# Graph attention with layer norm on one core: reciprocals spread by a DRAM round trip instead of TensorE, and division straight out of the weighed bank

## The reference

```
q, k, v = x Wq', x Wk', x Wv' + bv          (12 heads of 32)
a = q k' * 384**-0.5 + adj                  (per head, adj the same for all heads)
a = -inf in rows that are all 0;  a = softmax(a);  a = 0 where it is not a number
o = (a v, heads side by side) Wo' + bo
out = (r - mean(r)) / sqrt(var(r) + 1e-5),  r = x + o
```

## Time and profile before

| | us |
|---|---|
| median of 3 runs | 717.3 (717.02 to 719.97) |
| the profiled execution | 718.51 |
| its span, first to last instruction | 716.2 |
| PE busy in it | 698.7 |
| ACT busy | 613.8 |
| DVE busy | 600.1 |
| POOL busy | 487.2 |

### The profile page before, as it was taken

The page is one execution under the profiler, slowest core; times in us unless marked ns, Lnnn a source line. Parts: engine busy times, 40 slices in busy tenths (PEclk is TensorE's granted clock), DMA queues, the critical chain, the costliest instruction groups (busy, mean ns, idle before and its releaser), DMA issues.

```text
span 716.2 us, 23143 instructions
## 1 busy us (share of the span) xinstructions
PE 698.7 (98%) x7557; PEld 600.7 (84%) x7557; DVE 600.1 (84%) x2220; ACT 613.8 (86%) x1993; POOL 487.2 (68%) x548
## 2 busy tenths in 40 slices
PE   8999999999999999999999999999999999999895
PEld 8878888888888888888888888888898888888774
DVE  4898988889888889888889888889888889888973
ACT  4889988889988889988888988889888888898882
POOL 4767666677766678766677766678766677766452
PEclk9999999999999999999999999999999999999998
DMA  8475877787777687777787777787777777777672
GB/s 266 152 278 206 300 267 264 252 315 236 263 263 273 241 309 240 265 264 267 251 302 240 262 267 259 252 305 247 257 270 261 262 291 248 255 273 259 248 288 90
DMA packets 84008, 184.61 MB, mean 258 GB/s; under 512 B 4272, under 2 KB 42928, under 8 KB 75696
## 3 DMA queue, kind: packets, MB, share of 16 engines
q1 hardware_dynamic: 83888, 183.12, 72.3%
HBM read 103.42 MB, written 79.69 MB: 256 GB/s over the span
## 4 chain that ended last, share of the span: by engine, by line
PE 85%; DVE 5%; DMA 4%; issue 2%; POOL 2%; ACT 1%; SPq 0%; DVEq 0%; ACTq 0%; POOLq 0%
PE bank_b L787 34%; PE bank_c L787 16%; PE bank_a L877 12%; PE s_bank L836 11%; PE bank_t L847 8%; PE bank_c L858 2%; DVE neg L1192 2%; DMA sq_dram<-w_f 2%; DMA sq_probT<-sq_dram 2%; ACT prob L559 1%; PE bank_t L858 1%; DVE w_f L1209 1%; DMA xt<-in_xT 1%; POOL kq_lo L400 0%; DVE y L1292 0%
## 5 line engine op out<-in xcount | busy, mean ns | idle before, releaser
L559 ACT ACTIVATE prob<-neg,negmax 128x256 f32<-128x256 f32 x768 | 380.3, 500 | 51.8 <-DVE w_f L1209 34.3
L1192 DVE CUSTOM_DVE_ANT_0 neg<-s_bank,bias_sq 128x256 f32<-128x256 f32 x512 | 185.2, 414 | 49.0 <-issue 42.6
L1209 DVE STREAM_TRANSPOSE w_f<-prob 128x512 f32<-128x512 f32 x256 | 173.2, 696 | 0.7 <-ACT prob L559 0.7
L559 ACT ACTIVATION_READ_ACCUMULATOR prob<-neg,negmax 128x1 f32 x768 | 147.7, 192 | 0.0
L400 POOL TENSOR_TENSOR kq_lo<-kq,kq_hi 128x512 fp32r<-128x512 f32 x96 | 125.2, 1304 | 7.7
L398 POOL CAST kq_hi<-kq 128x512 fp32r<-128x512 f32 x96 | 60.2, 627 | 79.3 <-issue 73.9
L787 PE MATMUL bank_c<-xt_hi,w_hi 128*128 128x256 f32 x384 | 111.1, 289 | 1.0 <-DVE w_lo L1171 1.0
L787 PE MATMUL bank_c<-xt_hi,w_lo 128*128 128x256 f32 x384 | 108.3, 282 | 0.0
L787 PE MATMUL bank_c<-xt_lo,w_hi 128*128 128x256 f32 x384 | 108.3, 282 | 0.0
L1192 DVE CUSTOM_DVE_ANT_0 neg<-s_bank,bias 128x256 f32<-128x256 f32 x256 | 91.0, 420 | 15.2 <-PE s_bank L836 15.0
L847 PE MATMUL bank_t<-ident,prob 128*128 128x128 f32 x512 | 80.3, 279 | 0.7 <-ACT probT L569 0.7
(11 more groups left out here) (88 smaller groups left out, 1794.1 us busy)
## 6 DMA issues: line engine op xcount, KB each, us to landing
sq_dram<-w_f SPq DMA_DIRECT2D x64, 1024.0 KB, 4.5
sq_probT<-sq_dram SPq DMA_DIRECT2D x64, 1024.0 KB, 5.6
xt<-in_xT SPq DMA_DIRECT2D x32, 384.0 KB, 4.5
xr<-in_x SPq DMA_DIRECT2D x32, 384.0 KB, 6.2
out_y<-y_out SPq DMA_DIRECT2D x31, 384.0 KB, 3.0
bias<-in_adj SPq DMA_DIRECT2D x32, 256.0 KB, 3.2
w_f<-in_wkT SPq DMA_DIRECT2D x3, 192.0 KB, 4.5
w_f<-in_wqT SPq DMA_DIRECT2D x3, 192.0 KB, 5.0
```

The costliest lines, as they stand in the source:

```text
L559: nc.scalar.activation(prob[:, u % PROB_RING, k], neg[:, h, w.c], ACT.Exp, scale=-1.0, bias=negmax[t.p][:, w.c, h:h + 1], accum_out=sums[t ...
L1192: nc.vector.tensor_tensor_reduce(out=neg[:, h, w.c], in0=s_bank[h % JH][:, w.c, :], in1=by[t.p][:, w.c, :], scale=-1.0, scalar=BIG, op0=AL ...
L1209: nc.vector.transpose(sq_stage[w.g][:, :, a:a + PAIR, :, w.c].rearrange("p b h m s -> p (h m) b s"), prob[:, u % PROB_RING].rearrange("p k ...
```

## The change

It has four parts.

1. `widen_inv` (POOL) and `spread` (PE) go. `sums` is laid out so that the reciprocals of a row block, 24 columns of a 128 x 32 tile, can be transposed by DVE in blocks of 32 (`turn_inv`), stored to DRAM (`store_inv`, 16 KB) and loaded again by four DMAs, each of which gives 32 partitions the same row of 768 values (`load_inv`, inv_all).
2. `divide` now takes one g at a time, straight out of bank_a, and multiplies with inv_all. `save_o` goes, and o_n has two copies. The next weighing waits for the division (`o_n_ready`) instead of the copy.
3. v's second half is copied out by ACT (`copy_v`) and gets bv from POOL (`add_bv`); the first half stays with DVE. The flag moves from bank_a to bank_t.
4. The written order of all five engines is new, and the loop runs over batches 3 to 28. K01 is projected two batches ahead, x is loaded three ahead.

```diff
-    sums = [sb(f"sums{p}", [P, NT, H]) for p in range(2)]
+    sums = [sb(f"sums{p}", [P, JH, KC, NT]) for p in range(2)]
...
-    flags_at = bank_a[:, N:N + NT * H]
+    flags_at = t_flat[:, 0:NT * H]
...
+            def store_inv(t):
+                sp.wait_ge(inv_turned, t.count(1, 1))
+                apart(sp)
+
+                after(sp, inv_loaded[t.p], JH * (t.loads() - DMA))
+                sp.dma_start(inv_dram[t.p].rearrange("k b r -> b k r"),
+                             inv_t[:]).then_inc(inv_stored[t.p], DMA)
+
+            def load_inv(t):
+                sp.wait_ge(inv_stored[t.p], t.loads())
+                apart(sp)
+
+                after(sp, o_n_ready, t.count(KC, -KC))
+                for j in range(JH):
+                    row = inv_dram[t.p][KC * NT * j:KC * NT * (j + 1)].rearrange("k b r -> (k b r)")
+                    sp.dma_start(inv_all[t.p][HD * j:HD * (j + 1)].rearrange("p g n -> p (g n)"),
+                                 row.rearrange("(a n) -> a n", a=1).to_broadcast([HD, KC * N])
+                                 ).then_inc(inv_loaded[t.p], DMA)
...
+            def add_bv(t):
+                pool.wait_ge(b_loaded, 2 * DMA)
+                pool.wait_ge(v_copied, t.count(1, 1))
+                apart(pool)
+                nc.gpsimd.tensor_tensor(v[t.p][:, 1, :], v[t.p][:, 1, :], bv_all[:], ALU.add).then_inc(v_saved[1], 1)
...
-            def save_o(t, g):
-                act.wait_ge(pv_done[g], t.count(1, 1))
-
-                after(act, o_n_ready, t.count(2, -2))
-                nc.scalar.activation(o_raw[t.p][:, g, :], bank_at(t, f"PV{g}")[:, 0:N], ACT.Copy).then_inc(o_saved[g], 1)
+            def copy_v(t):
+
+                act.wait_ge(v_done, t.count(NT, 2))
+
+                for g in range(KC):
+                    after(act, pv_done[g], t.count(1, -1))
+                nc.scalar.activation(v[t.p][:, 1, :], bank_at(t, "V1")[:, 0:D], ACT.Copy).then_inc(v_copied, 1)
...
+            def turn_inv(t):
+                dve.wait_ge(inv_ready, t.count(1, 1))
+
+                if t.c >= 1:
+                    dve.wait_ge(inv_stored[1 - t.p], t.later(-1).loads())
+                apart(dve)
+                nc.vector.transpose(inv_t[:], inv[:]).then_inc(inv_turned, 1)
+
+            def divide(t, g):
+                dve.wait_ge(pv_done[g], t.count(1, 1))
+                if g == 0:
+                    dve.wait_ge(inv_loaded[t.p], JH * t.loads())
+
+                    after(dve, o_ready, t.count(2, -2))
+                    apart(dve)
+                nc.vector.tensor_tensor(o_n[t.p][:, g, :], bank_at(t, f"PV{g}")[:, 0:N], inv_all[t.p][:, g, :],
+                                        ALU.mult).then_inc(o_n_ready, 1)
```

More of the change, by code:

```diff
@@ new lines, in start @@
+                pe.wait_ge(kq_saved["Q12"], t2.count(1, 1))
+                project_kq(t3, "K01")
+                copied(t0, 11)
+                flag(t1)
+                pe.wait_ge(o_n_ready, t0.count(KC, 1))
+                weigh(t0, 1)
+                scores(t2, 0)
+                pe.wait_ge(flag_read, t1.count(1, 1))
+                transposes(t1, 8)
+                pe.wait_ge(o_n_ready, t0.count(KC, 2))
+                weigh(t0, 2)
+                pe.wait_ge(kq_saved["K2Q0"], t3.count(1, 1))
@@ L1069, in end @@
                 t31 = Batch(31)
+                scores(t29, 2)
+                copied(t28, 10)
+                transposes(t28, 11)
+                pe.wait_ge(kq_saved["K2Q0"], t30.count(1, 1))
+                project_v(t29, 1)
+                pe.wait_ge(kq_saved["K01"], t30.count(1, 1))
+                project_kq(t30, "Q12")
+                pe.wait_ge(o_n_ready, t28.count(KC, 1))
+                weigh(t28, 1)
+                pe.wait_ge(v_copied, t29.count(1, 1))
+                project_y(t27, 0)
```

794 lines of the change are left out of this document (427 added, 367 removed).

## The result

The changed kernel takes **747.8 us** (median of four runs, 740.70 to 753.59), the kernel before 717.2 in the same session: a ratio of 1.038, 95% interval [1.034, 1.041]. (Ratios are taken from the executions within 1.5% of a kernel's fastest alone: here three of the four, with a median of 746.4.) The forecast was 697 us with a range of 691 to 712. It is wrong, in sign too.

The account below looks back on a forecast made before the run. PE, busy all through the steady loop, was taken as the bound. From 718.5 us, 32 batches times 0.61 (19.5) and 1.0 for the end came off, giving 698.0; 1.2 less for the runs' median gave 697 us, range 691 to 712.

Parts of the forecast that it names:

- PE's step of 20.84: PE's new order in the steady loop, priced piece by piece: 20.84 us per step instead of 21.45, bounds 20.6 to 21.0.
- DVE's 0.4 us of margin: DVE's walk through the loop: no PE wait, the tightest place being the second division before weigh 2, 0.4 us to spare.
- part 6: Start and end of the kernel: 1.0 us off for the end, between 2.5 off and 2.5 on top.
- the factor of 32: The sum over the whole kernel: all 32 batches counted at 0.61 us saved each, 19.5 us.
- ACT and POOL were worth nothing: The two helper engines with copies and additions moved between them: enough time to spare, nothing counted.
- The second rival: DVE's margin is not there and PE waits at weigh 2: 707 us, or 717 if 0.6 us late; range 703 to 713.7, chance 0.14.
- part 4: The reciprocals' way through DRAM: 8.0 us from turn to landing, against about 9.3 that PE can bear.
- hidden, by 1.3 us: The reciprocals' way through DRAM costs PE nothing, with 1.3 us to spare.
- not full: DMA engines in the shorter step: 0.4 MB more per batch takes the busy share from 0.75 to about 0.83.
- the 1 MB load loses 1 us at most: SP's queue: the squares' load, waiting for a squares' store of 4.5 us, is delayed by at most 1 us.
- The first rival: Reciprocals reach DVE late, PE waits at weigh 1: 757 us, or 735 at a way of 10.5 us; chance 0.08 (slower).
- The rule on the store: Reciprocals' store to DRAM: slowest dimension 4, so 4 DMA engines; matters only if it lands after the squares ahead of the loads.

Follow-up runs that it names:

- e6: Changed kernel with the reciprocals' store and SP's waits kept, but the four loads left out from batch 3 on: 701.15 us.
- e1: Changed kernel with the reciprocals' store and four loads issued for the first two batches only: 700.28 us.
- e5: Changed kernel with, from batch 3 on, only the four loads, into a tile nobody reads, without the store and SP's waits for it: 747.52 us.
- e8: Changed kernel with the reciprocals' store and four loads issued by ACT on its own queue, SP's order otherwise kept: 851.11 us.
- e7: Changed kernel with SP's order changed: squares' load before the reciprocals' store, both x loads between store and four loads: 738.00 us.
- e12: Changed kernel with SP's whole step reordered so other transfers cover each landing, x transposed loaded four batches ahead; right data: 735.43 us.
- e9: As e5, changed kernel with loads into an unread tile and no store, but two of the four loads: 732.00 us.
- e11: As e5, but the 384 KB read as 128 different rows of x in one DMA to 128 partitions: 733.42 us.
- e18: Changed kernel with all orders and waits kept, but x's 384 KB for the residual not loaded from batch 2 on: 717.45 us.
- e17: Changed kernel with e12's order on SP and e14's on DVE, the four loads issued by GpSimd's queue in the loop: 743.40 us.
- e13: e12 with the four loads going to a tile nobody reads from batch 3 on, DVE dividing by batch 2's reciprocals: 729.12 us.
- e14: e12 with DVE inverting and turning the reciprocals earlier, behind two of the next batch's four bias additions: 735.48 us.
- e4: Changed kernel with the four loads ahead of the second load of squares in SP's order: 796.13 us.
- e2: Changed kernel with store and SP's waits kept, but from batch 3 on the four loads go to a tile nobody reads: 749.75 us.
- e15: e12 with the four loads made one DMA of 128 partitions, same bytes and rows, outermost dimension 4: 811.57 us.
- e3: Changed kernel with the reciprocals' store cut into four DMAs of 32 partitions: 761.86 us.

## Why the prediction was wrong

**What held.** PE's step of 20.84, with the spread's 0.59 us in it (20.83 and 20.86 in e6 and e1, PE busy 500 of 500 us), and DVE's 0.4 us of margin: in e6 the second division ends at 300.81 and the third weighing starts at 301.29. Without the loads no wait of PE shows, and both runs stand at 700 to 701 us, within the forecast's own 693 to 703 though 3 to 4 over its number. Those 3 to 4 lie outside the loop. Its 26 steps, 0.61 shorter each, give 15.9 of the 17.2 us between the profiled executions (718.51 and 701.33), which leaves 1.3 for start and end; part 6 and the factor of 32 counted 4.7. ACT and POOL were worth nothing, as said. The second rival (DVE's margin) did not occur.

**The step that failed** is in part 4: "its busy share of 0.75, in a shorter step too, to about 0.83: not full", and with it "hidden, by 1.3 us". The four loads were taken for traffic that costs nobody anything; they cost 46 us (e5 against e6). Three things in it were wrong.

*The size of the term.* Busy share times mean step is the time that a step's packets take on all 16 DMA engines; with shares read to two places it is good to about 0.1 us. Without the loads it is 0.77 x 20.83 = 16.0 us (e6), the same as before, 0.75 x 21.45 = 16.1. In the changed kernel it is 0.83 x 22.24 = 18.5. The forecast added 384 KB at the stage's mean rate per busy engine, 265/0.75 = 353 GB/s, so 1.1 us. They take **2.4 us**, over twice that. It is no constant of these bytes: with the same four loads it is 1.6 in e8 (0.66 x 26.7), 1.8 in e7 (0.81 x 22.0) and 2.2 in e12 (0.83 x 22.0). In e9 half of the loads adds 0.80 x 22.18 - 16.0 = 1.7; in e11 the same bytes in one transfer 0.81 x 22.24 - 16.0 = 2.0.

Of the 2.4 us, the loads' own packets are 128 x 195 ns / 16 = 1.6; with e11's 126 ns they would be 1.0, about what was forecast. The other 0.8 are packets of the old transfers that became longer: those of 1536 bytes (x for the residual and the output) from 71 ns in e6 to 83, those of 2048 (the squares' loads) from 101 to 107.

In the forecast's step of 20.84 the share would have to be 0.89, not 0.83. It reads 0.83 because the step grew. A packet's time counts its waiting too (119 ns at the least, 195 on average), so the 18.5 is no pure demand; but e6 and before agree at two step lengths. And e18, with e6's bytes but four narrow loads in the place of one wide one, has 0.79 x 21.62 = 17.1: for the same bytes the narrow form adds 1.0 us.

*What "not full" means.* No run got past 0.83 and 279 GB/s between 100 and 600 us: the changed kernel 273, e17 276, e12 277, e7 and e13 278, e14 279, with several orders and two queues. The rate needed in a step of 20.84 is e6's 275 plus 384 KB in 20.84 us (19), 294 GB/s. So a mean of 0.83 was the most that was reached here, not 1.00. That it is the capacity of the engines is not shown, and it isn't the whole: e9 (0.80, 266 GB/s) and e18 (0.79, 263) stay below it, and below e6's 275, and are still 31 and 13 to 16 us slower than e6. There landings close a loop with SP's waits, as e14's chain has it, and a reordering moved 12 us.

*Landings taken as constants.* The 5.6 us of the earlier trace rows was kept for the squares' load, and 4.5 for their store ("the 1 MB load loses 1 us at most"). The squares' store went to 7.9, and from e6 (5.3) to there only the loads and DVE's wait for them were added. The store itself did not slow down: one of its packets, 8192 bytes, takes 313 ns on average, 315 in e6. But from its issue to its first packet lie 3.4 and 3.6 us (medians of the two stores of a step), 0.8 and 1.5 in e6. SP runs late and issues its transfers closer together, so what went ahead is still under way: the first store goes 0.8 us behind x at 307.30, and 4.4 us behind it at 315.89 in e6. Since their load waits for that store on SP, and store, loads, x and the next squares' store stand behind it, each longer landing comes back a few places later in the queue. The loads land 4.7 us after issue, where 1.4 was counted; with the squares' load behind them, as in e4, it is 2.3.

**The first rival** named late reciprocals and gave 735 to 757 us. The number covers the result and the mechanism is seen in the late step (13.3 us). But that the number fits is luck, as the mechanism is the smaller part of the cause: e13 prices the arrival at 6 us in e12's order, and e2, without it, is no faster than the changed kernel. Its reasoning, that the store or the squares come late at given landings, lacked what made them late. Its chance of 0.08 rested on that same constant.

**The rule on the store.** By the Trainium skill's page "DMA: Bandwidth & Descriptors", section "Why a DMA increments its semaphore by 16 and not by 1", the store runs on 4 engines. e6 shows that store and waits cost 0.9 us there, on however many engines. In e4 and e7, where SP has no store of squares to wait for between the reciprocals' store and the loads, it waits 4.1 and 3.1 us each time for its landing, so it is cheap only while something else covers it. The rule would have been of use for the loads: e15, whose outermost dimension is 4, is the slowest form of them.

**Still open**: how far the longer landings come from the engines' capacity and how far from SP's loop of waits, and how the rest (e18's 13 to 16 us above e6) parts into transfers to 32 partitions and SP's order. A version with fewer or wider loads that computes the reference was not found.

## What to carry to other kernels

When a change adds traffic beside a full compute engine, work out what all DMA engines are asked for in the *new* step, price the added transfers by their own shape and not by the mean rate, and don't count on a mean share that no run of the kernel has reached: here steps grew at 0.79 and 0.80 already, and none got past 0.83. A landing time read at one load is no constant: where one queue waits for landings in order, run the walk again with each landing half as long again. And to tell a late result from crowding, send the traffic to a tile nobody reads.

## What the runs showed of the hardware

- The squares' store of 1 MB lands in 4.5 us at a share of 0.75 and 5.3 at 0.77 (e6), 7.9 at 0.83 in the changed kernel and 8.4 at 0.82 in e5. But the share doesn't set it: with all the loads and another order it is 5.1 at 0.81 (e7) and 6.6 at 0.83 (e12).
- The bias of 256 KB lands in 3.2, 6.1, 8.2 and 9.2 us in the same first four. The step from 3.2 is mostly its new place behind out and a store of squares: it is 5.7 in e1.
- Packets of 3072 bytes take 195 ns on average when they go to 32 partitions at a time (161 in e8, at a share of 0.66) and 126 in one transfer to 128; reading one row again and again or 32 different ones makes no difference (195 and 197).
- Three ways of moving the same 384 KB: four DMAs of 32 partitions 747 us, one of 128 different rows 733, one whose outermost dimension is 4, 812 in the order of e12, where four DMAs of 32 take 735.
- Four issues of a DMA cost 1.72 us of SP, 1.73 of ACT (e8) and 2.10 of POOL (e17).
- Cutting a 16 KB store in four cost 14 us (e3).
